# Masks of the attention scores added by VectorE instead of TensorE, with the PSUM banks split 3 and 2

## What is computed

```python
# xf: x normalised by groups, as (B, T * F, D)
s = jnp.einsum('bhqe,bhke->bhqk', q, k) * scale
mask = i[:, None] <= i[None, :] if lookahead else i[:, None] >= i[None, :]
s = jnp.where(mask, s, jnp.finfo(s.dtype).min)
p = jax.nn.softmax(s, axis=-1)
return jnp.einsum('bhqk,bhke->bhqe', p, v)
```

## Time and profile before

| | us |
|---|---|
| median of 3 runs | 3200.27 |
| lowest and highest | 3194.33, 3206.62 |
| the profiled execution | 3198.2 |
| its span, first to last instruction | 3196.4 |
| TensorE matmuls busy in it | 3094.5 |
| VectorE busy | 1947.2 |
| ScalarE busy | 1600.9 |
| GpSimd busy | 1271.4 |

### The profile page before, as it was taken

How to read it: one execution, slowest core, us unless ns; L and a number is a source line. 1 busy time by engine, 2 the same in 40 slices (tenths; PEclk the granted TensorE clock), 3 DMA queues, 4 the chain that set the end, 5 groups by cost and what they waited for, 6 DMA issues and landing times.

```text
span 3196.4 us, 42508 instructions
## 1 busy us (share of the span) xinstructions
PE 3094.5 (97%) x14500; PEld 2512.7 (79%) x14500; DVE 1947.2 (61%) x3574; ACT 1600.9 (50%) x3188; POOL 1271.4 (40%) x1004
## 2 busy tenths in 40 slices
PE   6999999999999779999999999999999999999998
PEld 4788888888888658787878787888888788878886
DVE  6222212411121188887787788778877887788874
ACT  4210212211121056766666666666666766676665
POOL 4000001100000145656565556555655555565554
PEclk9999999999999979999999999999999999999999
DMA  3546734633533553533353334324433443344330
GB/s 129 174 128 156 210 125 119 197 122 102 139 119 98 116 113 82 109 78 72 80 106 77 69 86 101 79 67 92 100 73 67 98 94 73 70 101 88 73 73 20
DMA packets 352199, 325.50 MB, mean 102 GB/s; under 512 B 276225, under 2 KB 276225, under 8 KB 339713
## 3 DMA queue, kind: packets, MB, share of 16 engines
q1 hardware_dynamic: 352000, 323.02, 40.8%
HBM read 205.52 MB, written 117.44 MB: 101 GB/s over the span
## 4 chain that ended last, share of the span: by engine, by line
PE 56%; DVE 8%; issue 1%; DMA 0%; ACT 0%; SPq 0%; POOL 0%; DVEq 0%; ACTq 0%
PE rows L1229 12%; PE scores L1197 7%; PE acc L1211 7%; PE acc L1215 7%; PE turning L1164 7%; PE acc L1213 7%; PE scores L1192 7%; DVE o_full L1133 2%; DVE part_max L1085 2%; PE turning L1174 1%; PE scores L1195 1%; DVE diagonal L889 1%; DVE inv L1112 1%; DVE inv L1119 1%; DVE p_low L878 0%
## 5 line engine op out<-in xcount | busy, mean ns | idle before, releaser
L878 POOL TENSOR_TENSOR p_low<-probs,p_high 128x512 fp32r<-128x512 f32 (+2 forms) x960 | 1198.9, 1260 | 854.0 <-ACT p_high L1015 558.5
L1011 ACT ACTIVATE probs<-scores 128x512 f32<-128x512 f32 (+3 forms) x1280 | 684.5, 535 | 589.9 <-PE scores L1197 574.2
L1085 DVE TENSOR_REDUCE part_max<-turning 128x1 f32<-128x512 f32 (+3 forms) x1280 | 766.1, 603 | 213.2 <-PE turning L1164 190.1
L1015 ACT ACTIVATE p_high<-scores 128x512 fp32r<-128x512 f32 (+3 forms) x1280 | 679.8, 531 | 0.0
L418 DVE TENSOR_TENSOR stage_l<-proj,stage_h 128x512 fp32r<-128x512 f32 x192 | 132.1, 690 | 698.4 <-ACT stage_h L410 670.2
L410 ACT ACTIVATE stage_h<-proj 128x512 fp32r<-128x512 f32 x192 | 114.7, 599 | 829.5 <-PE proj L341 443.7
L1164 PE MATMUL turning<-k,q 128*128 128x512 f32 (+3 forms) x1280 | 472.0, 371 | 18.5 <-DMA k<-qk_l 17.3
L1197 PE MATMUL scores<-q,k 128*128 128x512 f32 (+3 forms) x1280 | 488.5, 382 | 0.0
L1192 PE MATMUL scores<-q,k 128*128 128x512 f32 (+3 forms) x1280 | 470.2, 367 | 1.2 <-ACT p_high L1015 1.1
L1211 PE MATMUL acc<-p_high,v 128*128 128x512 f32 (+3 forms) x1280 | 466.3, 364 | 5.2 <-DVE p_low L878 5.0
L1215 PE MATMUL acc<-p_low,v 128*128 128x512 f32 (+3 forms) x1280 | 468.3, 366 | 0.0
(11 more groups left out here) (93 smaller groups left out, 4310.6 us busy)
## 6 DMA issues: line engine op xcount, KB each, us to landing
qk_h<-stage_h SPq DMA_DIRECT2D x128, 256.0 KB, 2.5
qk_l<-stage_l SPq DMA_DIRECT2D x128, 256.0 KB, 3.0
q<-qk_h SPq DMA_DIRECT2D x64, 512.0 KB, 6.2
k<-qk_h SPq DMA_DIRECT2D x64, 512.0 KB, 7.9
xs<-xT SPq DMA_DIRECT2D x40, 512.0 KB, 4.7
w_raw<-wqk SPq DMA_DIRECT2D x32, 512.0 KB, 4.0
v_h<-stage_h SPq DMA_DIRECT2D x64, 256.0 KB, 2.6
v_l<-stage_l SPq DMA_DIRECT2D x64, 256.0 KB, 3.0
```

What stands on the lines that cost most here:

```text
L878: eng.tensor_tensor(p_low[:, n % 4, part], probs[:, n % 4, part], p_high[:, n % 4, part].bitcast(F32), ALU.subtract).then_inc(done, 1)
L1011: nc.scalar.activation(probs[:, n % 4, 0:cols], scores[n % 2][:, 0:cols], ACT.Exp, scale=SCALE).then_inc(exp_done, 1)
L1015: nc.scalar.activation(p_high[:, n % 4, 0:cols], scores[n % 2][:, 0:cols], ACT.Exp, scale=SCALE).then_inc(high_act, 1)
L1085: nc.vector.tensor_reduce(part_max[:, s % 2, at, m:m + 1], bank_of[:, 0:cols], AX.X, ALU.max).then_inc(max_read, 1)
```

## The change

The third matmul of a score tile on the diagonal goes. Instead VectorE adds the mask to the 128 columns in the `scores` bank, at the place of that score tile in its own list, before any `p_low` of that step, and signals `score_masked`; ScalarE waits for that instead of for TensorE. The banks are split anew: three for scores, two for `turning`. Tile n now waits until ScalarE has read tile n - 3, and a matmul into `turning` until the use two places earlier has been read. AHEAD becomes 4, the places for probabilities five, and the shift of stage 2 moves from step 6 to step 7. Since tile n is now issued at step n - 4, tile 12 (first of stage 2) goes out at step 8 and tile 24 (first of stage 3) at step 20.

```diff
-AHEAD = 3
+AHEAD = 4
+P_PLACES = 5
+SCORE_BANKS = 3
+TURN_BANKS = 2
-SHIFT_SLOT = {2: 6, 3: 19, 0: 24, 1: 32}
+SHIFT_SLOT = {2: 7, 3: 19, 0: 24, 1: 32}
@@ banks
-        scores = [bank(f"scores{n}") for n in range(2)]
-        turning = [bank(f"turning{n}") for n in range(3)]
+        scores = [bank(f"scores{n}") for n in range(SCORE_BANKS)]
+        turning = [bank(f"turning{n}") for n in range(TURN_BANKS)]
@@ wait_turn
-            if place >= 3:
-                before, head, unit = taken_by[place - 3]
+            if place >= TURN_BANKS:
+                before, head, unit = taken_by[place - TURN_BANKS]
@@ scalar, scores
-                    act.wait_ge(scored, count(i, p, S_TILES, n + 1))
-
-                    wait_low(act, i, p, n - 4)
+                    if square is None:
+                        act.wait_ge(scored, count(i, p, S_TILES, n + 1))
+                    else:
+                        act.wait_ge(score_masked, count(i, p, 4 * STAGES, at + 1))
+
+                    wait_low(act, i, p, n - P_PLACES)
@@ vector, scores
+                    s, at, _, _, col, _, square = score_tile(kind, n)
+                    if square is not None:
+                        dve.wait_ge(scored, count(i, p, S_TILES, n + 1))
+                        own = score_bank(i, p, n)[:, square - col:square - col + P]
+                        nc.vector.tensor_tensor(own, own, (below if kind == LB else beyond)[:, :].bitcast(F32),
+                                                ALU.add).then_inc(score_masked, 1)
@@ tensor, scores
-                    if (n - 2) % 4 in HIGH_ACT:
-                        wait_one(pe, high_act, HIGH_ACT, i, p, n - 2)
-                    else:
-                        reached(pe, exp_done, count(i, p, S_TILES, n - 1))
+                    wait_high(pe, i, p, n - SCORE_BANKS)
-                    if square is not None:
-
-                        nc.tensor.matmul(to[:, square - col:square - col + P], eye[:, :],
-                                         (below if kind == LB else beyond)[:, :], start=False, stop=False)
```

More of the change, by code:

```diff
@@ L727, in attend @@
         v = sb("v", [P, 2, TOK, VC], F32R)
-        probs = sb("probs", [P, 4, NQ])
-        p_high = sb("p_high", [P, 4, NQ], F32R)
-        p_low = sb("p_low", [P, 4, NQ], F32R)
+        probs = sb("probs", [P, P_PLACES, NQ])
+        p_high = sb("p_high", [P, P_PLACES, NQ], F32R)
+        p_low = sb("p_low", [P, P_PLACES, NQ], F32R)
         acc_s = sb("acc_s", [P, NQ])
@@ L772, in attend @@
         scored = sem("scored")
+        score_masked = sem("score_masked")
         exp_done = sem("exp_done")
@@ L832, in turn_bank @@
         def turn_bank(step, i, p, n):
-            return turning[places[step, 2 * i + p, n] % 3]
+            return turning[places[step, 2 * i + p, n] % TURN_BANKS]
         def wait_turn(eng, step, i, p, n):
             place = places[step, 2 * i + p, n]
-            if place >= 3:
-                before, head, unit = taken_by[place - 3]
+            if place >= TURN_BANKS:
+                before, head, unit = taken_by[place - TURN_BANKS]
                 if before == "max":
@@ L847, in count, with score_bank @@
             return i * (2 * per_head) + (p * per_head + n)
+        def score_bank(i, p, n):
+            return scores[count(i, p, S_TILES, n) % SCORE_BANKS]
         def taken(members, n):
@@ L875, in low_part @@
             wait_high(eng, i, p, n)
-            reached(eng, weighed, count(i, p, S_TILES, n - 3))
-            eng.tensor_tensor(p_low[:, n % 4, part], probs[:, n % 4, part],
-                              p_high[:, n % 4, part].bitcast(F32), ALU.subtract).then_inc(done, 1)
+            reached(eng, weighed, count(i, p, S_TILES, n - P_PLACES + 1))
+            eng.tensor_tensor(p_low[:, n % P_PLACES, part], probs[:, n % P_PLACES, part],
+                              p_high[:, n % P_PLACES, part].bitcast(F32), ALU.subtract).then_inc(done, 1)
         def first_head(i, p):
@@ L1006, in do @@
                 elif step == "scores":
[L1007 to L1011 removed]
+                    s, at, _, _, _, cols, square = score_tile(kind, n)
+                    if square is None:
[3 more added lines that the diff above has]
+                    wait_low(act, i, p, n - P_PLACES)
+                    nc.scalar.activation(probs[:, n % P_PLACES, 0:cols], score_bank(i, p, n)[:, 0:cols], ACT.Exp,
                                          scale=SCALE).then_inc(exp_done, 1)
                     if n % 4 in HIGH_ACT:
[L1014 to L1015 removed]
+                        reached(act, weighed, count(i, p, S_TILES, n - P_PLACES + 1))
+                        nc.scalar.activation(p_high[:, n % P_PLACES, 0:cols], score_bank(i, p, n)[:, 0:cols], ACT.Exp,
                                              scale=SCALE).then_inc(high_act, 1)
@@ L1176, in do @@
                 elif step == "scores":
-                    s, at, qb, j, col, cols, square = score_tile(kind, n)
+                    s, at, qb, j, col, cols, _ = score_tile(kind, n)
                     if n == 0:
@@ L1208, in do @@
                     wait_low(pe, i, p, n)
-                    high, low = p_high[:, n % 4, 0:cols], p_low[:, n % 4, 0:cols]
+                    high, low = p_high[:, n % P_PLACES, 0:cols], p_low[:, n % P_PLACES, 0:cols]
                     sums = acc[s % 2]
```

8 lines of the change are left out of this document (4 added, 4 removed).

## The result

The changed kernel takes 3277.19 us (median of 6 runs, 3265.91 to 3280.43) against 3196.98 us for the kernel before beside it. The ratio is 1.0242, with a 95% interval of 1.0227 to 1.0257: 80 us slower. The forecast was 3322 us, 124 slower, with a range from 3241 to 3421.

A forecast was written before the change was run, and what follows sets the result against it. TensorE, 99% busy in steady heads, was taken as the bound. Rest 50.3 + stretch 14.9 + second place 1.6 + clock 0.7 = 67.5 us a head, 4.0 above 63.5; times 31 gives 3322 us, range 3241 to 3421.

The forecast's parts named there:

- The stretch: Steps 0 to 8, from max unit 23 to tile 12: 14.9 us (13.5 to 15.9), where it was 12.52.
- The waits at steps 6 to 8: TensorE waits about 1 us at each step for a turning bank, unit 27 being queued behind the divide.
- The rest of the head: The head outside the stretch: 50.98 us before, less 1.34 for masks and 0.28 for the Wo wait, plus 0.93: 50.3.
- The second place: Steps 16 to 20: waits for the bank of stage 3's shift and at tile 24, 1.6 us (up to 2.5).
- The clock: Behind the new waits the granted clock can fall to half: 0.7 us a head, from 0 to 2.
- The masks on TensorE: Each of 16 mask matmuls a head costs 0.11 us, columns and weight load: 1.8 us a head, 57 us in all.
- The two waits can go: TensorE's waits at the shift of stage 2 (0.87 us, 0.10 at restart) and the first Wo piece (0.28) can go.
- The two turning banks: With two banks TensorE can't be three uses ahead; its waits at steps 6 to 8 are inside the 14.9 us.
- The masks as a part of the cause: In steps 0 to 8 the masks of tiles 8 to 11 lengthen VectorE's list from 11.7 to 12.9 us.

The follow-up runs named there:

- a1: The changed kernel with the score masks added by TensorE again (three scores banks, two turning banks, four tiles ahead kept): 3288.24 us.
- a4: The changed kernel without any mask on the score tiles, neither on VectorE nor on TensorE: 3278.32 us.
- b3: The kernel before without any mask on the score tiles: 3160.49 us.
- c2: The kernel before with four tiles ahead, five places and the shift of stage 2 at step 7; TensorE masks and bank split kept: 3209.42 us.
- c3: The changed kernel with two banks of scores and three turning banks, as in the kernel before: 3259.05 us.
- c1: The kernel before with the bank split alone changed, to three banks of scores and two turning banks: 3237.32 us.
- d2: The changed kernel with one added VectorE operation a head, about 0.6 us, behind the mask of tile 9 in step 5: 3352.34 us.
- d1: The changed kernel with the roundings, the first twelve Wo pieces and the first addition one step later: 3292.87 us.
- a2: The kernel before with VectorE adding the score masks as the one change (two scores banks, three turning banks, three tiles ahead): 3245.09 us.
- e1: The kernel before with roundings, first twelve Wo pieces and first addition a step later, and the shift of stage 2 at step 7: 3263.11 us.
- a3: The changed kernel with the shifts of stages 2 and 3 a step earlier (steps 6 and 18), the diagonal of stage 3 at 16: 3267.57 us.

## Why the prediction was right in direction and too large

It had the sign, the place and the mechanism of the main wait: VectorE fills steps 0 to 8, TensorE waits there at units 29 to 31, at the shift, and at tile 12 for ScalarE's copy. All of these are in the profile of after. Step by step:

- **The stretch**, 14.9 us, measured 12.98, below its low end of 13.5. This term was mis-sized. VectorE came to unit 23 0.54 us after TensorE started it, where I had estimated 1.1 (0.56 less). A mask in the middle of VectorE's list occupies it for 0.20 us (2023.39 to 2023.59), and I had charged its length, 0.29 (0.3 less for the four). The rounding before mask 11 occupied VectorE for 0.60 where I left 1.1 from before (0.5 less). The second rounding, which I also counted in the list, stands behind mask 11 and isn't in the 11.7 us that I started from. The divide occupied it for 1.55 where I took about 1.85 (0.3 less). The way from mask 11 to tile 12 took 1.15 (2027.86 to 2029.01), not 1.3. These make 1.8 of the 1.9 us.
- **The waits at steps 6 to 8**, foretold at about 1 us each and inside the stretch, were 0.25 at unit 29, 0.73 at unit 30 and 0.30 at unit 31, with 0.43 at the shift. TensorE is busy 96% of a head, where 92% was foretold.
- **The rest of the head**, 50.3, measured 65.26 - 12.97 - 0.95 = 51.3 with the second place taken out. I had missed the shift of stage 0, 0.47 us, which waits for its bank; the rest are small restarts.
- **The second place**, 1.6, measured 0.44 at the shift of stage 3 and 0.51 at tile 24. The place and the two waits were right; the low end, 1.1, was nearer. The divide there stayed at 0.84 us, so the contention that I allowed for wasn't met.
- **The clock**, 0.7 a head, measured 0.36. It falls in 7 of 30 heads and costs 1.5 us each.
- **The masks on TensorE**: 0.11 us each, 1.8 us a head. A head after is 1.80 us longer with 3.3 us more of waits, so the work is 1.5 us shorter, with some restarts in it; a1 against a4 without their waits gives 1.7. So a mask costs more than its 128 columns (0.06 us each, 1.0 a head). The page "TensorE: Matmul & The Clock Gate" of the Trainium skill (section "Back-to-back issue gap") gives 81 ns, 1.3 us a head, which is too low here. What I hadn't said is that in the kernel before more than a third of it turns to wait (b3).
- **"The two waits can go"**: wrong for the shift. A step later it waits 0.43 us in the changed kernel, for its bank, but 1.56 in c2 with TensorE's masks. The wait of the first Wo piece did go.
- **The two turning banks**: called inside the stretch and not added. c3 agrees, stretch 12.92 against 12.98. But with three tiles ahead they cost 1.1 us a head by themselves (c1), so they aren't free where VectorE's list is the same.
- **The masks as a part of the cause**: the sum had them lengthen the stretch by 1.2 us. They do stand in the list, but a4 shows that without them the stretch is 12.68 and the head no shorter, since GpSimd then comes in beside `p_low` and the diagonal. This step failed: but for 0.4 us off the divide, the durations of VectorE's operations in the trace of before were treated as fixed.

The errors of the terms are -1.9, -0.65 and -0.35 us for the stretch, the second place and the clock, and +1.0 for the rest of the head. Together that is the 1.9 us between 67.5 and 65.6. That the last one offsets a third of the others is luck.

What stays open: each part alone costs (masks 1.33, banks 1.13, tiles ahead with the later shift 0.55 us a head), and together they cost 2.16, less than the sum of 3.01. That contention with GpSimd is what ties them is shown by the rows for a4 and d2. For the others the lengths of the same operations follow GpSimd by the same rule (below), but that this makes up the 0.85 us wasn't tested. No run took GpSimd's work away.

## What to carry to other kernels

Work that is moved from the bound engine to one with slack costs what the list at its new place costs: 0.6 us cost nothing in step 13 and 2.7 us in step 5 of the same head, with the same mean load. Where two engines share something, the length of an operation belongs to the schedule it was measured in; a sum should carry its quiet length and its worst one, since taking work out may lengthen the work that stays. And a list moved for one engine moves for all: d1 freed VectorE and blocked ScalarE.

## What the runs showed of the hardware

- A VectorE operation with two SBUF inputs that starts beside a GpSimd `p_low` takes longer, by the time that GpSimd's still has to run, less 0.13 us. Between 1300 and 3100 us of the changed kernel 387 such operations (the diagonal, `p_low` and `o_low` of 512 columns, the divides) started with no GpSimd operation running, and all took their quiet length: 0.68 us, or 0.41 for a divide of 256 columns. 137 were longer, every one by that sum to 0.01 us, and 28 that met at most the last 0.16 us of a GpSimd operation were not. The same holds in before, a1, a2, a4, b3, c1, c2, c3, d2 and e1. In a1 and c2 one divide a head starts 0.01 us behind GpSimd's operation and keeps its 0.41 us; there GpSimd's takes 1.57 to 1.59 us instead of 1.29. So the diagonal takes anything from 0.68 to 1.75 us and a divide 0.41 to 1.52. The maximum of 512 columns, whose only input is in PSUM, stayed at 0.62 to 0.69 us, and an addition in PSUM at 0.28 to 0.30, in every run. The page "SBUF — State Buffer" of the Trainium skill (section "SBUF: two separate sides") describes such an exclusion; these lengths agree with it.
- The sum of the waits doesn't tell how often the clock falls. In the 30 heads the granted clock fell to 0.50 for 3.4 us 7 times in the changed kernel (4.3 us of waits a head), 14 times in a1 (3.0 us), 11 in a4 (4.3 us) and never in a3 (4.4 us). Each fall of 3.4 us costs 1.5 us, as TensorE has work in it.
- A wait of TensorE costs about 0.10 us more than its idle time, in the slower start of the matmul behind it (2045.40 to 2045.73 in the earlier trace rows is 0.33 us, not 0.23; in the trace of the changed kernel 2026.41 to 2026.72 is 0.31, and 2029.01 to 2029.35 is 0.34).
